# Cross-attention and routed FFN on one core: where twelve output-projection pieces, four residual adds and one key product stand in the steps of a batch

## The chip, the cores and the metric

One Trainium2 chip, one of its cores. The metric is the device time of the kernel in microseconds (us). The engines are TensorE (PE in the rows; PEld is its weight load), VectorE (DVE), ScalarE (ACT), GpSimd (POOL) and SyncE (SP), which here only issues transfers.

## The reference

```python
# B=8 batches of S=512 tokens, H=512, 16 heads of 32, context width 128
x = x + xattn(layernorm(x), ctx)          # causal attention, keys and values from ctx
x = x + ffn(layernorm(x))                 # router of 8 experts, top 2 by output column

def xattn(q, latent):
    qp = q @ Wq.T;  k, v = split(latent @ Wkv.T)
    scores = (qh @ kh.T) / sqrt(32), masked to the causal part
    out = softmax(scores) @ vh
    return out @ Wout.T
```

Every matrix product of float32 is made of three products of a high and a low part.

## The kernel before, in words

The first third of the span is the attention, the rest the router and the experts. The change touches only the attention.

The attention runs over 8 batches. A batch is four groups `c` = 0 to 3 of four heads each (called first to fourth group here), and a group is eight steps `v` = 0 to 7 (`UNITS`). The order of work is written out by hand: each engine's `body` is one Python loop over `c` and `v`, and small tables and functions say which extra pieces stand in which step. Engines meet only through semaphores. In each step TensorE makes, in this order:

- `shifted_scores` (L705): the transposed scores of one block of keys for two heads, into the one pair of banks `e_ps`. It waits until ScalarE has taken the exponential (L1095) of the step before. In step 0 it also waits for `rows_in`: two rows of row maxima that SyncE has copied into the stacked operands (L380).
- The score product of the second head for the group ahead (L672), whose row maxima VectorE takes (L1390; L1384 where the mask is added on TensorE by L678). TensorE may write a score bank again when `negmax` has counted the maxima that read it.
- Extra pieces: a quarter of a query product in steps 0, 2, 3 and 4; in step 1 the rest of the previous group's values and sums (L721, L741); in step 7 the first two blocks of values (L721, L733); a key product (`keys`) in step `key_step(c)`.
- The output projection of the **previous** batch (`project_out`, three matmuls at L261 to L263 with the operands `wo_h`, `wo_l`, `oT_h`, `oT_l`). A batch has 4 row blocks `i` of 4 pieces. All four pieces of a block add up in the one bank `j_ps[0]`. The first piece of the next block waits (`take(0, ...)`, `freed`) for `x1_ok`, which counts VectorE's `residual` (L1426): the add of the old `x` that empties this bank.
- The score product of the first head (or the masked pair), and in step 5 `turn_maxima` (L687), which transposes the maxima of the next group.

After L687 ScalarE and VectorE split the transposed maxima (L1020, `lo_shift` at L1399, which stands behind the maxima of step 5), SyncE copies the two rows (L380), and step 0 of the next group may begin.

Which piece stands where: `OUT_FIRST` gives the first of four steps in a row for each block. `summed_block` gives the step of the residual, one after the block's last piece; VectorE makes it ahead of the maxima of that step. The key product of the fourth group stands in step 5 and its low part (`lo_of`, L1372) in step 6 (`key_rest`), ahead of the maxima. Keys of the first and fourth group use `j_ps[0]` too, the same bank as the output projection. The first batch has no projection, and the last batch has tables of its own (`OUT_FIRST_LAST`), which the change leaves alone, so six of the eight batches have the four blocks of the table `OUT_FIRST`.

Of the kernel before, what the change touches and what calls it, by code (L numbers as in the profile page):

```python
# [34 lines left out]
UNITS = QB * 2  # L35
# [10 lines left out]
def build(nc, x, ctxT, wqT, wkvT, woT, routerT, router_b, expertT, expert_b, out):  # L46
    ctx = ExitStack()
    with ctx:
# [170 lines left out]
        def some(value):  # L219

            return not isinstance(value, int) or value > 0
# [43 lines left out]
        def target(c, v):  # L265

            k = v + LEAD
            return 1 + k // UNITS, k % UNITS

        def masked(c, v):  # L270

            return v in (3, 4) or c == 0 and v > 4

        def block_of(v):

            return QB - 1 - v // 2
# [18 lines left out]
        def key_bank(c):  # L295

            return 1 if c in (1, 2) else 0

        def key_step(c):

            return 6 if c in (1, 2) else 5

        OUT_FIRST = ((1, 0), (1, 6), (2, 3), (3, 0))
        OUT_FIRST_LAST = ((1, 0), (1, 4), (2, 0), (2, 4))

        def key_rest(c):

            return {0: (0, 5), 1: (1, 7), 2: (2, 7), 3: (3, 6)}[c]

        FIX_EXPERT = 1  # L310
        EXPERT_FIXES = 2 * NE
# [6 lines left out]

        def out_block(c, v, last):

            for i, (c0, v0) in enumerate(OUT_FIRST_LAST if last else OUT_FIRST):
                chunk = (c - c0) * UNITS + v - v0
                if 0 <= chunk < KC:
                    return i, chunk
            return None

        def summed_block(c, v, last):

            step = c * UNITS + v - (0 if last else 1)
            at = out_block(step // UNITS, step % UNITS, last)  # L330
            return at[0] if at and at[1] == KC - 1 else None


# [275 lines left out]
        def _(pe):  # L609
# [197 lines left out]
            def body(b, first, more, further):  # L807
# [7 lines left out]
                for c in range(KC):  # L815
# [3 lines left out]
                    def project(v):  # L819
                        i, chunk = out_block(c, v, last)  # L820
                        if chunk == 0:
                            take(0, "WO", (b - 1) * QB + i)
                        project_out(b - 1, i, chunk, 0)
# [5 lines left out]
                    for v in range(UNITS):  # L829
# [19 lines left out]
                        if v == key_step(c) and ahead:  # L849
                            take(key_bank(c), "K", n + AHEAD)  # L850
                            keys((c + AHEAD) % KC, b if c == 0 else b + 1, key_bank(c))
# [127 lines left out]
        def _(act):  # L979
# [101 lines left out]
            def body(b, first, more, further):  # L1081
                last = not more
                for c in range(KC):
                    n = b * KC + c
                    ahead = more or c == 0
                    for v in range(UNITS):
# [22 lines left out]
                        if v == key_step(c) and ahead:  # L1109
                            hi_of(n + AHEAD, KH, "k", key_bank(c))  # L1110
# [212 lines left out]
        def _(dve):  # L1323
# [23 lines left out]
            def block_statistics(b, i):  # L1347
                if i == 0:
                    dve.wait_ge(s["x_in"], (b + 1) * 16)
                statistics(b * QB + i, i, xt[:, i, :], "ln")  # L1350
                mean_variance(b * QB + i, i, "ln")
# [5 lines left out]
            def turned_tokens(g, i, bank):  # L1357
                dve.wait_ge(s["xT_hi"], g + 1)
                cols = slice(i * P, (i + 1) * P)
                dve.tensor_tensor(xnT_l[:, :, cols], j_ps[bank][:].rearrange("p (k q) -> p k q", k=KC),  # L1360
                                  f32(xnT_h[:, :, cols]), ALU.subtract).then_inc(s["xT_lo"], 1)

            def lo_of(n, part, name, bank):

                dve.wait_ge(s[name + "_hi"], n + 1)
                full, hi = j_ps[bank], f32(qk[:, part - 1])
                if name == "q":

                    dve.scalar_tensor_tensor(qk[:, part], full[:], SCALE, hi, ALU.mult, ALU.subtract)\
                        .then_inc(s["q_lo"], 1)  # L1370
                else:
                    dve.tensor_tensor(qk[:, part], full[:], hi, ALU.subtract).then_inc(s["k_lo"], 1)  # L1372

            def maxima(n, c, v, mask=False):

                u = n * UNITS + v
                i, pair = block_of(v), v % 2
                if v == 0 and some(n - 1):

                    dve.wait_ge(s["turned"], n - 1)  # L1380
                if mask:
                    at = 2 * pair * QB + i
                    dve.wait_ge(s["scores"], 2 * u + 2)
                    dve.tensor_reduce(nmax[:, c % 2, at:at + QB + 1:QB], s_ps[:, :, 0:(i + 1) * P], AX_X, ALU.max,  # L1384
                                      negate=True).then_inc(s["negmax"], 2)
                for j in range(0 if mask else 2):
                    at = (2 * pair + j) * QB + i
                    dve.wait_ge(s["scores"], 2 * u + 1 + j)
                    row = s_ps[:, j, 0:(i + 1) * P]
                    dve.tensor_tensor_reduce(row, row, future[:, S - (i + 1) * P:S], -1.0, -MASKED, ALU.add, ALU.min,  # L1390
                                             accum_out=nmax[:, c % 2, at:at + 1]).then_inc(s["negmax"], 1)

            def lo_shift(n):

                dve.wait_ge(s["nm_hi"], n + 1)
                if some(n * (16 * SHIFT_ROWS)):
                    dve.wait_ge(s["rows_in"], n * (16 * SHIFT_ROWS))
                rows = slice(0, HC * QB)
                dve.tensor_tensor(nm_l[rows, :], r_ps, f32(nm_h[rows, :]), ALU.subtract).then_inc(s["nm_lo"], 1)  # L1399

            def refined(n, c):

                dve.wait_ge(s["recips"], n + 1)
                o = o_sb[OUT_BUF[c]]
                dve.scalar_tensor_tensor(d_ps[:], d_ps[:], -1.0, o[:], ALU.mult, ALU.mult).then_inc(s["refined"], 1)
                dve.wait_ge(s["refined"], 2 * n + 1)
                dve.scalar_tensor_tensor(o[:], d_ps[:], 2.0, o[:], ALU.add, ALU.mult).then_inc(s["refined"], 1)

            def scaled(n, c, totals=o_ps):

                dve.wait_ge(s["refined"], (n + 1) * 2)
                o = o_sb[OUT_BUF[c]]
                dve.tensor_tensor(o[:], totals[:], o[:], ALU.mult).then_inc(s["o_ok"], 1)
# [9 lines left out]
            def residual(b, i, bank):  # L1423
                dve.wait_ge(s[f"xr_in{i % 2}"], (b * (QB // 2) + i // 2 + 1) * 16)
                dve.wait_ge(s["wo_mm"], b * QB + i + 1)
                dve.tensor_tensor(xr[:, i % 2, :], j_ps[bank][:], xr[:, i % 2, :], ALU.add).then_inc(s["x1_ok"], 1)  # L1426
# [32 lines left out]
            def body(b, first, more, further):  # L1459
                last = not more  # L1460
                for c in range(KC):
                    n = b * KC + c
                    ahead = more or c == 0
                    for v in range(UNITS):
                        if v == TURN + 1 and (more or c < KC - 1):
                            lo_shift(n + 1)
                        if not (first and c == 0):
                            if v == REFINED:
                                refined(n - 1, (c - 1) % KC)
                            if v == SCALED:  # L1470
                                scaled(n - 1, (c - 1) % KC)
                        i = None if first else summed_block(c, v, last)
                        if i is not None:
                            residual(b - 1, i, 0)
                        if (c, v) == key_rest(c) and ahead:
                            lo_of(n + AHEAD, KL, "k", key_bank(c))
                        if c == 0 and more:
                            for i in TURNED.get(v, ()):
                                turned_tokens((b + 1) * QB + i, i, 1 - i % 2)
                        if (c, v) in STATISTICS and further:  # L1480

                            block_statistics(b + 2, STATISTICS.index((c, v)))
                        g, vv = target(c, v)
                        if more or c + g < KC:
                            maxima(n + g, (c + g) % KC, vv, masked(c, v))
                        if QUERY.get(v) == KC - 1 and ahead:
                            lo_of(n + AHEAD, QL, "q", 1)
                        if last:
                            for k, q in FIX_EARLY.get((c, v), ()):
                                fix_router(k, q)  # L1490
                        if last and (c, v) in LO_EARLY:
                            lo_router(LO_EARLY.index((c, v)))
# [71 lines left out]
            def lo_router(e):  # L1564
                dve.wait_ge(s["fw_hi"], e + 1)
                dve.tensor_tensor(w_l[:, e], w_raw[:, e], f32(w_h[:, e]), ALU.subtract).then_inc(s["fw_lo"], 1)
# [392 lines left out]
```

## Time and profile before

| | |
|---|---|
| time, median of 3 runs | 1985.36 us (1985.3 to 1987.68) |
| the profiled execution, its own time | 1986.06 us |
| its span | 1984.3 us |
| TensorE busy | 1910.6 us, 96% |
| VectorE busy | 1432.1 us, 72% |
| ScalarE busy | 1039.0 us, 52% |
| GpSimd busy | 850.5 us, 43% |
| TensorE weight load busy | 1514.7 us, 76% |

The span runs from the first to the last instruction of one profiled execution, and its own time is that of the same execution. Busy shares are means over stages with different limits; the last product of scores and values in the attention starts at 614.8 us. A batch in its middle repeats itself within some hundredths of a microsecond, so that one batch can be read for all. The rows below are of the batch from 266.90 to 339.60 us and, where a step without a projection piece is wanted, of the first batch.

### The profile page before, as it was taken

The page shows a single profiled execution, that of the slowest core. Times are in us where ns is not written, and L with a number is a line of the kernel's source. Part 1 is how long each engine was busy: PE and PEld are TensorE (multiplying, and loading weights), DVE is VectorE, ACT ScalarE, POOL GpSimd, SP SyncE. Part 2 cuts the span into 40 slices and gives each one's busy share as a digit, 9 for nine tenths or more (in the row PEclk, how much of TensorE's full clock was granted, in tenths as well). Part 3 has the DMA queues.
Part 4 walks back from the last instruction along what each step waited for, and adds up shares of the span by engine and source line. Part 5 has one row for each costly group of instructions (what it writes and reads, how often), then busy time and mean ns, then how long its engine had stood idle before and what let it go on. Part 6 is the DMA issues. An engine that isn't in the chain of part 4 may idle for free.

```text
span 1984.3 us, 30426 instructions
## 1 busy us (share of the span) xinstructions
PE 1910.6 (96%) x9772; PEld 1514.7 (76%) x9772; DVE 1432.1 (72%) x2840; ACT 1039.0 (52%) x2062; POOL 850.5 (43%) x1016
## 2 busy tenths in 40 slices
PE   4899999999998999999999999999999999999999
PEld 3666766777765788888888888778888888888887
DVE  5667667767668658787888888477777777777732
ACT  2566566566554347877777787533443333344400
POOL 5577777777674135456445435102321111232100
PEclk8999999999999999999999999999999999999999
DMA  5454555455466468787856555822232222223111
GB/s 166 121 125 130 137 144 128 124 149 134 108 166 229 159 229 274 231 271 221 254 203 217 190 186 196 313 85 79 94 118 85 80 95 85 80 86 124 49 42 33
DMA packets 103693, 294.54 MB, mean 148 GB/s; under 512 B 13777, under 2 KB 14801, under 8 KB 98482
## 3 DMA queue, kind: packets, MB, share of 16 engines
q1 hardware_dynamic: 91394, 209.44, 33.1%
q10 hardware_dynamic: 8880, 67.37, 10.5%
q0 software_dynamic: 3328, 16.78, 3.7%
q8 instruction: 25, 0.41, 0.1%
q14 instruction: 66, 0.54, 0.1%
HBM read 150.31 MB, written 109.16 MB: 131 GB/s over the span
## 4 chain that ended last, share of the span: by engine, by line
PE 83%; DVE 7%; DMA 3%; issue 2%; POOL 2%; ACT 2%; ACTq 0%; SPq 0%; DVEq 0%; POOLq 0%
PE pair L261 20%; PE pair L263 20%; PE pair L262 20%; PE pair L672 3%; PE ps L721 3%; PE ps L261 3%; PE pair L705 3%; PE ps L262 3%; PE ps L263 3%; DMA w_raw<-w_fix 1%; DVE pair L1390 1%; PE ps L741 1%; DVE w_raw L1525 1%; POOL pT L1836 1%; PE ps L902 1%
## 5 line engine op out<-in xcount | busy, mean ns | idle before, releaser
L261 PE MATMUL pair<-w_h,hT 128*128 128x512 f32 x1920 | 751.7, 392 | 6.4 <-ACT w_h L1201 3.6
L263 PE MATMUL pair<-w_h,hT 128*128 128x512 f32 x1920 | 748.5, 390 | 0.0
L262 PE MATMUL pair<-w_l,hT 128*128 128x512 f32 x1920 | 748.3, 390 | 0.0
L1908 POOL TENSOR_TENSOR logits<-logits,second 128x512 f32<-128x512 f32 x224 | 298.6, 1370 | 590.9 <-DVE second L1605 590.6
L261 PEld LDWEIGHTS pair<-w_h,hT 128*128 128x128 f32 x1920 | 361.4, 188 | 81.9 <-issue 5.8
L263 PEld LDWEIGHTS pair<-w_h,hT 128*128 128x128 f32 x1920 | 361.1, 188 | 75.8
L262 PEld LDWEIGHTS pair<-w_l,hT 128*128 128x128 f32 x1920 | 361.3, 188 | 74.1
L1708 DVE SCALAR_TENSOR_TENSOR xb<-pair,c_all,xb 128x512 f32<-128x512 f32 x256 | 191.7, 749 | 195.6 <-PE pair L263 189.5
L1095 ACT ACTIVATE pT<-pair,zero 128x1024 f32<-128x1024 f32 (+3 forms) x256 | 202.6, 792 | 192.0 <-PE pair L705 183.6
L1390 DVE CUSTOM_DVE_ANT_0 pair<-pair,future 128x256 f32<-128x256 f32 (+3 forms) x340 | 184.1, 554 | 124.3 <-PE pair L672 115.9
L1191 ACT ACTIVATE w<-tree 128x512 f32<-128x512 f32 x32 | 20.3, 635 | 388.6 <-DVE tree L1607 388.6
L672 PE MATMUL pair<-qk_st 96*128 96x256 f32 (+3 forms) x512 | 159.3, 341 | 21.7 <-DVE nmax L1390 7.8
L1836 POOL TENSOR_SCALAR_AFFINE_SELECT pT<-pT 128x256 f32<-128x256 f32 x248 | 105.6, 426 | 137.1 <-ACT pT L1095 136.8
L1659 DVE SCALAR_TENSOR_TENSOR scrap<-ps,w 128x512 bf16<-128x512 f32 x224 | 152.9, 683 | 0.8 <-ACT w L1194 0.8
L1170 ACT ACTIVATE over<-over 128x512 f32<-128x512 f32 x224 | 141.7, 633 | 7.0
L1167 ACT ACTIVATE junk<-over 128x512 bf16<-128x512 f32 x224 | 141.5, 632 | 7.1
L1653 DVE SCALAR_TENSOR_TENSOR ps<-logits,ps 128x512 f32<-128x512 f32 x192 | 133.2, 694 | 16.3
L672 PEld LDWEIGHTS pair<-qk_st 96*128 96x128 f32 x512 | 96.8, 192 | 62.9 <-issue 23.9
L705 PE MATMUL pair<-qk_st 98*128 98x256 f32 (+3 forms) x512 | 133.2, 341 | 8.3 <-ACT pT L1095 6.3
L1162 ACT ACTIVATE over<-logits 128x512 f32<-128x512 f32 x224 | 130.2, 624 | 8.6 <-POOL logits L1908 7.6
L1828 POOL TENSOR_TENSOR acc<-acc,pT 128x512 f32<-128x512 f32 (+1 forms) x124 | 125.2, 1010 | 10.3
L1823 POOL TENSOR_TENSOR acc<-pT,pT 128x768 f32<-128x768 f32 x62 | 114.4, 1846 | 5.2
(166 smaller groups left out, 2609.7 us busy)
## 6 DMA issues: line engine op xcount, KB each, us to landing
logits<-lg_all ACTq DMA_DIRECT2D x32, 1792.0 KB, 8.9
qk_st<-qk SPq DMA_DIRECT2D x372, 128.0 KB, 2.4
lg_all<-ev_a SPq DMA_DIRECT2D x31, 768.0 KB, 8.5
lg_all<-ev_b SPq DMA_DIRECT2D x31, 768.0 KB, 3.8
xb<-x SPq DMA_DIRECT2D x64, 256.0 KB, 2.9
hT_all<-hT SPq DMA_DIRECT2D x32, 512.0 KB, 4.3
hT<-hT_all SPq DMA_DIRECT2D x32, 512.0 KB, 4.0
xt<-in_x SPq DMA_DIRECT2D x8, 1024.0 KB, 5.4
```

The lines of the kernel that those rows point to most:

```text
L261: pe.matmul(dst, lh, rh, start=start, stop=False)
L262: pe.matmul(dst, lh, rl, start=False, stop=False)
L263: return pe.matmul(dst, ll, rh, start=False, stop=stop)
L672: mm = pe.matmul(s_ps[:, j, 0:w], qk_st[c][0:STACK, 0, hh, i * P:w], qk_st[c][0:STACK, 1, hh, 0:w], start=True, stop=not mask)
L705: mm = pe.matmul(dst[:, j, 0:w], qk_st[c][0:STACK + SHIFT_ROWS, 1, hh, kb * P:(kb + 1) * P], qk_st[c][0:STACK + SHIFT_ROWS, 0, hh, kb * P: ...
L1095: act.activation(pT[kb][:, pair:pair + 2, :], src[:, :, 0:S - kb * P], ACT.Exp, bias=zero[:])\
L1167: act.activation(junk[:], over[j][:], ACT.Sign, accum_out=sign_sum[:, i, e:e + 1])\
L1170: act.activation(over[j][:], over[j][:], ACT.Tanh, scale=0.5, accum_out=tanh_sum[:, i, e:e + 1]).then_inc(s["first_step"], 1)
L1390: dve.tensor_tensor_reduce(row, row, future[:, S - (i + 1) * P:S], -1.0, -MASKED, ALU.add, ALU.min, accum_out=nmax[:, c % 2, at:at + 1]).t ...
L1659: dve.scalar_tensor_tensor(scrap[:, e % 2, :], taken_ps[e % 2], 1.0, w2[:], ALU.min, ALU.mult, accum_out=c_taken[:, i, e - 1:e]).then_inc( ...
L1708: dve.scalar_tensor_tensor(xb[i][:], l_ps[e % 4], c_all[:, t, e:e + 1], xb[i][:], ALU.mult, ALU.add).then_inc(s["acc"], 1)
L1908: pool.tensor_tensor(logits[t % 2][:, e - 1, :], logits[t % 2][:, e - 1, :], second[:], ALU.subtract)\
```

## The change

Blocks 0 to 3 are the row blocks of the output projection. `(c, v)` is group index and step.

| | before | after |
|---|---|---|
| block 0, pieces | (1,0) (1,1) (1,2) (1,3) | the same |
| block 0, residual | (1,4), ahead of the maxima | (1,4), behind the maxima |
| block 1, pieces | (1,6) (1,7) (2,0) (2,1) | (1,6) (1,7) (2,0) (2,2) |
| block 1, residual | (2,2), ahead | (2,3), behind |
| block 2, pieces | (2,3) (2,4) (2,5) (2,6) | (2,4) (2,5) (2,6) (2,7) |
| block 2, residual | (2,7), ahead | (3,0), behind |
| block 3, pieces | (3,0) (3,1) (3,2) (3,3) | (3,1) (3,2) (3,3) (3,4) |
| block 3, residual | (3,4), ahead | (3,5), ahead |
| keys of the fourth group | (3,5), low part (3,6) | (3,6), low part (3,7) |

Counted by step, (2,1), (2,3) and (3,0) lose a piece and (2,2), (2,7) and (3,4) get one. Nothing is added or left out.

```diff
         def key_step(c):
 
-            return 6 if c in (1, 2) else 5
-
-        OUT_FIRST = ((1, 0), (1, 6), (2, 3), (3, 0))
+            return 6 if c else 5
+
+        OUT_AT = (((1, 0), (1, 1), (1, 2), (1, 3)), ((1, 6), (1, 7), (2, 0), (2, 2)),
+                  ((2, 4), (2, 5), (2, 6), (2, 7)), ((3, 1), (3, 2), (3, 3), (3, 4)))
+        SUMMED_AT = ((1, 4), (2, 3), (3, 0), (3, 5))
...
-            return {0: (0, 5), 1: (1, 7), 2: (2, 7), 3: (3, 6)}[c]
+            return {0: (0, 5), 1: (1, 7), 2: (2, 7), 3: (3, 7)}[c]
...
-            for i, (c0, v0) in enumerate(OUT_FIRST_LAST if last else OUT_FIRST):
+            if not last:
+                for i, steps in enumerate(OUT_AT):
+                    if (c, v) in steps:
+                        return i, steps.index((c, v))
+                return None
+            for i, (c0, v0) in enumerate(OUT_FIRST_LAST):
...
-            step = c * UNITS + v - (0 if last else 1)
-            at = out_block(step // UNITS, step % UNITS, last)
+            if not last:
+                return SUMMED_AT.index((c, v)) if (c, v) in SUMMED_AT else None
+            at = out_block(c, v, last)
...
-                        i = None if first else summed_block(c, v, last)
-                        if i is not None:
-                            residual(b - 1, i, 0)
+                        summed_i = None if first else summed_block(c, v, last)
+                        sooner = last or (c, v) == (3, 5)
+                        if summed_i is not None and sooner:
+                            residual(b - 1, summed_i, 0)
...
                             maxima(n + g, (c + g) % KC, vv, masked(c, v))
+                        if summed_i is not None and not sooner:
+                            residual(b - 1, summed_i, 0)
```

In the rows below, line numbers of the changed kernel are 8 higher than those of before (L1434 is the residual L1426, L713 is L705 and so on).

VectorE, third group, from step 2 to step 4, before: the residual of block 1 stands ahead of the second pair of maxima.

```order
L1426 TENSOR_TENSOR xr<-ps,xr 128x512
L1390 ISA pair,nmax<-pair,future 128x256
L1390 ISA nmax 128x1
L1390 ISA pair,nmax<-pair,future 128x256
L1390 ISA nmax 128x1
L1405 SCALAR_TENSOR_TENSOR ps<-ps,o_sb_90 128x512
L1407 SCALAR_TENSOR_TENSOR o_sb_90<-ps,o_sb_90 128x512
L1384 TENSOR_REDUCE nmax<-pair 128x2
L1413 TENSOR_TENSOR o_sb_90<-ps,o_sb_90 128x512
L1384 TENSOR_REDUCE nmax<-pair 128x2
```

The same place in the changed kernel:

```order
L1398 ISA pair,nmax<-pair,future 128x256
L1398 ISA nmax 128x1
L1398 ISA pair,nmax<-pair,future 128x256
L1398 ISA nmax 128x1
L1413 SCALAR_TENSOR_TENSOR ps<-ps,o_sb_90 128x512
L1415 SCALAR_TENSOR_TENSOR o_sb_90<-ps,o_sb_90 128x512
L1392 TENSOR_REDUCE nmax<-pair 128x2
L1434 TENSOR_TENSOR xr<-ps,xr 128x512
L1421 TENSOR_TENSOR o_sb_90<-ps,o_sb_90 128x512
L1392 TENSOR_REDUCE nmax<-pair 128x2
```

The residual now stands behind the two operations that refine the reciprocals (L1413, L1415 there) and behind the masked maxima of step 3 (L1392).

TensorE, third group, from `shifted_scores` of step 7 to that of the fourth group's step 0, before:

```order
L705 MATMUL pair<-qk_st_75 128x128 x2
L672 MATMUL pair<-qk_st_73 128x512
L721 MATMUL ps<-pT_77,v_sb 32x512 x4
L733 MATMUL ps<-pT_77,ones 32x128 x4
L721 MATMUL ps<-pT_78,v_sb 32x384 x4
L671 ISA
L672 MATMUL pair<-qk_st_73 128x384
L696 REGISTER_ALU
L705 MATMUL pair<-qk_st_76 128x512 x2
```

And in the changed kernel:

```order
L713 MATMUL pair<-qk_st_75 128x128 x2
L680 MATMUL pair<-qk_st_73 128x512
L729 MATMUL ps<-pT_77,v_sb 32x512 x4
L741 MATMUL ps<-pT_77,ones 32x128 x4
L729 MATMUL ps<-pT_78,v_sb 32x384 x4
L261 MATMUL ps<-wo_h,oT_h 128x512
L262 MATMUL ps<-wo_l,oT_h 128x512
L263 MATMUL ps<-wo_h,oT_l 128x512
L679 ISA
L680 MATMUL pair<-qk_st_73 128x384
L704 REGISTER_ALU
L713 MATMUL pair<-qk_st_76 128x512 x2
```

The last piece of block 2 has come in between the values of step 7 (L729) and the score product.

VectorE, fourth group, from the masked maxima of step 3 to the split of the turned maxima (`nm_l`), before:

```order
L1384 TENSOR_REDUCE nmax<-pair 128x2
L1413 TENSOR_TENSOR o_sb_91<-ps,o_sb_91 128x512
L1426 TENSOR_TENSOR xr<-ps,xr 128x512
L1384 TENSOR_REDUCE nmax<-pair 128x2
L1369 SCALAR_TENSOR_TENSOR qk<-ps,qk 128x512
L1390 ISA pair,nmax<-pair,future 128x512
L1390 ISA nmax 128x1
L1390 ISA pair,nmax<-pair,future 128x512
L1390 ISA nmax 128x1
L1399 TENSOR_TENSOR nm_l<-ps,nm_h 16x128
```

And in the changed kernel:

```order
L1392 TENSOR_REDUCE nmax<-pair 128x2
L1421 TENSOR_TENSOR o_sb_91<-ps,o_sb_91 128x512
L1392 TENSOR_REDUCE nmax<-pair 128x2
L1377 SCALAR_TENSOR_TENSOR qk<-ps,qk 128x512
L1434 TENSOR_TENSOR xr<-ps,xr 128x512
L1398 ISA pair,nmax<-pair,future 128x512
L1398 ISA nmax 128x1
L1398 ISA pair,nmax<-pair,future 128x512
L1398 ISA nmax 128x1
L1407 TENSOR_TENSOR nm_l<-ps,nm_h 16x128
```

The residual of block 3 has moved from ahead of the masked maxima of step 4 to ahead of the maxima of step 5, right behind the low part of the queries (L1377).

## Rows read from the trace of the kernel before

**Rows 1.** Third group: length; busy PE, PEld, DVE, ACT, POOL (instructions); clock, DMA share, GB/s.

```profile
305.04:322.59 17.55, 17.34 (x119) 12.64 (x119) 13.72 (x40) 9.71 (x14) 12.98 (x22) 1.00 0.49 121
```

**Rows 2.** Timeline of PE, second group's step 7, third group: start us, us, engine, line.

```profile
301.65 0.34 PE L705 MATMUL pair<-qk_st 98*128 98x128 f32 x2
...
305.04 0.63 PE L705 MATMUL pair<-qk_st 98*128 98x512 f32 x2
...
307.24 0.63 PE L705 MATMUL pair<-qk_st 98*128 98x512 f32 x2
...
310.33 0.52 PE L705 MATMUL pair<-qk_st 98*128 98x384 f32 x2
...
314.34 0.45 PE L705 MATMUL pair<-qk_st 98*128 98x256 f32 x2
...
315.33 0.39 PE L261 MATMUL ps<-wo_h,oT_h 128*128 128x512 f32 x1
...
316.41 0.45 PE L705 MATMUL pair<-qk_st 98*128 98x256 f32 x2
...
319.91 0.34 PE L705 MATMUL pair<-qk_st 98*128 98x128 f32 x2
...
322.59 0.63 PE L705 MATMUL pair<-qk_st 98*128 98x512 f32 x2
```

**Rows 3.** Timeline of PE, fourth group of the same batch.

```profile
324.80 0.63 PE L705 MATMUL pair<-qk_st 98*128 98x512 f32 x2
...
326.97 0.50 PE L261 MATMUL ps<-wo_h,oT_h 128*128 128x512 f32 x1
...
327.89 0.52 PE L705 MATMUL pair<-qk_st 98*128 98x384 f32 x2
...
332.12 0.45 PE L705 MATMUL pair<-qk_st 98*128 98x256 f32 x2
...
333.50 0.51 PE L705 MATMUL pair<-qk_st 98*128 98x256 f32 x2
334.06 0.50 PE L261 MATMUL ps<-ctx_h,wkv_h 128*128 128x512 f32 x1
...
339.60 0.72 PE L705 MATMUL pair<-qk_st 98*128 98x512 f32 x2
```

**Rows 4.** Timeline of PE, first batch (no projection), fourth group, steps 0 to 2.

```profile
106.12 0.72 PE L705 MATMUL pair<-qk_st 98*128 98x512 f32 x2
...
108.05 0.72 PE L705 MATMUL pair<-qk_st 98*128 98x512 f32 x2 [0.16 <-ACT pT L1095]
...
110.53 0.52 PE L705 MATMUL pair<-qk_st 98*128 98x384 f32 x2
```

**Rows 5.** Timeline of DVE, third and fourth group, same batch as rows 2 and 3.

```profile
316.68 0.42 DVE L1384 TENSOR_REDUCE nmax<-pair 128x2 f32<-128x256 f32 x1 [1.03 <-PE pair L678]
317.02 0.68 DVE L1369 SCALAR_TENSOR_TENSOR qk<-ps,qk 128x512 fp32r<-128x512 f32 x1
...
325.65 0.57 DVE L1390 CUSTOM_DVE_ANT_0 pair<-pair,future 128x384 f32<-128x384 f32 x1
...
332.73 0.68 DVE L1413 TENSOR_TENSOR o_sb<-ps,o_sb 128x512 f32<-128x512 f32 x1
333.32 0.68 DVE L1426 TENSOR_TENSOR xr<-ps,xr 128x512 f32<-128x512 f32 x1
...
335.41 0.70 DVE L1390 CUSTOM_DVE_ANT_0 pair<-pair,future 128x512 f32<-128x512 f32 x1 [0.48 <-PE ps L687]
...
336.67 0.27 DVE L1399 TENSOR_TENSOR nm_l<-ps,nm_h 16x128 fp32r<-16x128 f32 x1
```

**Rows 6.** Transfers of the shift rows, fourth group: the issue, and issue to landing.

```profile
337.63 0.59 SPq L380 DMA_DIRECT2D qk_st<-nm_l  x1
...
DMA to landing us min/median/max: 1.8/1.8/1.8
```

## The prediction

> **What bounds the kernel now.** I read the page first: TensorE is busy nearly all the time, so the question is what a step of the attention waits for. Busy time by stretch says less than it seems: in the third group of a batch TensorE shows 17.34 of 17.55 us busy, VectorE 13.72, at a granted clock of 1.00 [rows 1]. So I took the timeline of TensorE and read the start of every L705, which opens a step. The difference of two neighbours is what a step costs, waits included, and the same step with and without a projection piece gives the price of a piece there. Then I read VectorE's timeline beside it, since TensorE stops where `negmax` or `x1_ok` is late, and SyncE's issues, since a group cannot begin before its two shift rows have landed.
>
> What the reader is to see. Step 1 lasts 3.09 us with a piece (307.24 to 310.33) [rows 2] and 2.48 without (108.05 to 110.53) [rows 4]. Step 0 lasts 2.21 us with a piece (322.59 to 324.80) [rows 2, 3] and 1.93 without (106.12 to 108.05), and there the next step waits for ScalarE's exponential [rows 4], so part of the piece is covered. Step 4 lasts 2.07 us with a piece (314.34 to 316.41) [rows 2] and 1.38 without (332.12 to 333.50) [rows 3]. Step 7 lasts 3.39 us with a piece (301.65 to 305.04) and 2.68 without (319.91 to 322.59) [rows 2]. The price of a piece is thus 0.28 us in step 0, 0.61 in step 1, 0.69 in step 4 and 0.71 in step 7. The change moves pieces out of the cheap places and into the dear ones.
>
> The fourth group ends on something else. VectorE's split of the maxima ends at 336.94 (336.67 and 0.27) [rows 5], the second shift row is issued at 337.63 and lands 1.8 later, at 339.43 [rows 6], and the next group's step 0 starts at 339.60 [rows 3]. So there the end of the group follows L1399 at 2.66 us, whatever TensorE does meanwhile. From step 5 to the end that group takes 6.10 us (333.50 to 339.60) [rows 3] with one key product in it, the third group 6.18 (316.41 to 322.59) [rows 2] with three extra pieces: TensorE has room there.
>
> **The change part by part, for one batch.** No instruction and no transfer is added or removed, so every term is a place.
>
> *Block 0, second group.* Its residual goes behind the maxima of step 4. The next steps there are held by the exponentials and the low part of the queries, and VectorE does the same sum of work before the maxima of step 5. I take 0.
>
> *Third group, step 1* loses its piece: 3.09 to 2.48, a gain of 0.61.
>
> *Third group, steps 2 to 4* last 6.08 us together now (310.33 to 316.41) [rows 2], with pieces in steps 3 and 4. After the change the pieces are in steps 2 and 4, which would be no longer. But the piece of step 4 is the first of block 2 and must wait for the residual of block 1, and this now stands behind the refined reciprocals and the masked maxima. I time this chain on the fourth group, whose step 2 has a piece already: step 2 starts at 327.89 [rows 3], and what stands behind the masked maxima of step 3 (there L1413) starts at 332.73 [rows 5], 4.84 later. In its place comes the residual, 0.68 long, and TensorE goes on 0.06 after a residual: L1426 ends at 334.00 [rows 5] and the product that waited for it starts at 334.06 [rows 3]. So the piece starts 4.84 + 0.68 + 0.06 = 5.58 after step 2's start. From that piece to the next step is 1.08 (315.33 to 316.41) [rows 2]. The stretch becomes 6.66, a loss of 0.58. It eats what step 1 gave. Bounds: without a wait 6.08 or a little less (0), and 0.7 more if VectorE is late there by one operation.
>
> *Third group, steps 5 to 7.* Steps 5 and 6 keep their pieces. Step 7 gets one behind the values: 2.68 to 3.39, a loss of 0.71. The rows of the third group have landed long before. Bounds: 0 if something covers it, 0.71 as read in the second group. I take 0.71, since that step is the same but for the group. The residual that stood in this step is gone from it, but nobody waited there for it.
>
> Third group together: -0.61 + 0.58 + 0.71 = +0.68 us.
>
> *Fourth group, step 0* loses its piece: 2.21 to 1.93, a gain of 0.28. *Step 1* keeps one, now the first of block 3, which waits for the residual of block 2 behind the maxima of step 0. The second of these maxima starts 0.85 after step 1's start (325.65 against 324.80), VectorE's operations of that kind follow at 0.6 or less, and the residual with its 0.68 ends some 2.1 to 2.2 after it; the piece stands at 2.17 (326.97) [rows 3, 5]. It just fits, and I take 0.
>
> *Fourth group, step 4* gets a piece: 1.38 to 2.07, a loss of 0.69. Step 5 then starts 0.41 later than now.
>
> *Fourth group, steps 5 to 7.* The end is that of L1399, so I follow VectorE from the start of step 5. Now the maxima of step 5 start 1.91 after it (335.41 against 333.50) [rows 3, 5]. Then: the masked maxima of step 4 start 0.27 after it (316.68 against 316.41, a step 4 with a piece), the low part of the queries 0.34 later (317.02) [rows 2, 5], and two operations, this one and the residual, at the distance of 0.59 that L1413 and L1426 show (332.73 to 333.32) [rows 5]: 0.27 + 0.34 + 2 x 0.59 = 1.79. That is 0.12 sooner. Before, TensorE's key product had itself waited for the residual (until 334.06) [rows 3] and held up the score; that goes away. Maxima, L1399, rows and landing follow as before. The key product now lies in step 6 beside this leg; TensorE's room there covers it, and if it did not it would cost the 0.69 of a product of three matmuls.
>
> Fourth group together: -0.28 + 0.69 - 0.12 = +0.29 us.
>
> *SyncE and the key operands.* The residuals of blocks 1 and 3 end later, and their stores stand ahead of the shift rows in SyncE's queue. Block 3's ends 1.88 after step 5's start and L1399 some 1.4 later, so the store of one issue is out before. The key's low part comes two maxima later, about 1.26 us (335.41 to 336.67) [rows 5]. Behind it are twelve copies of heads, at 0.59 an issue and 1.8 to land [rows 6] 8.9 us, read first after step 5 of the next group, which starts over 11 us into a group (305.04 to 316.41) [rows 2]. Both cost 0.
>
> **Sum.** 0.68 + 0.29 = 0.97 us a batch, and six batches have these tables: +5.8 us. The first batch only gets the moved keys, in the same cover, and the last nothing. The profiled execution took 1986.06 us around its span of 1984.3; with 5.8 it would be 1991.9. The median of the runs is 0.7 lower, 1985.36, and gives 1991.2 us.
>
> **The rivals.** What tells a measurement of this kernel from no change is 0.2%, 4.0 us or 0.66 us a batch.
>
> *A. TensorE does not wait at the third group's step 4.* If VectorE gets the residual of block 1 done in time, the 0.58 goes: 0.39 a batch, +2.3, 1987.7 us, no change that can be told. It decides from a wait shorter by 0.31. Against it stands the order of the rows: two refinements and the masked maxima are ahead of it, and they are timed. Chance 0.10.
>
> *B. The piece in step 7 is covered.* TensorE's weight loads fill only 12.64 of 17.55 us in the third group, against 17.34 of its matmuls [rows 1]. If the engine has that room, the piece of step 7 costs nothing: 0.26 a batch, +1.6, 1987.0 us. Against it, a piece in this very step of the second group costs 0.71 [rows 2]. Chance 0.13. The Trainium skill, Perfetto Trace Analysis, section Identifying the Most-Contended Engine, speaks for this rival: it calls matmul busy time a poor measure because matmuls are pipelined, and wants the busy share of the weight loads instead. By that rule the engine has headroom in which moved work should vanish; by the steps with and without a piece it has not, in steps 1, 4 and 7, and I go by those.
>
> *C. More waits.* At the fourth group's step 1 the margin is nil. If the residual of block 2 slips behind one more operation of some 0.5 us, each batch loses that too: +8.8, 1994.2 us. Chance 0.12.
>
> *D. Faster.* It would need A and B at once and more: together they give 0.97 - 0.58 - 0.71 = -0.32 a batch, -1.9 us, still within 0.2%. Only if the fourth group's piece in step 4 were covered too (-0.69) would it be -6.1, 1979.3. Chance 0.06. That the new order does not take effect is excluded by the order of instructions, but its effect may be lost in what I do not see: 0.03.
>
> My forecast has 0.56. The range goes from 1986.8, which takes in A and B, to 1994.6, which takes in C. Slower has my forecast and C, 0.68; the same A, B and the rest, 0.26; faster 0.06.
>
> **What the profile of the changed kernel would show.** L705 starts of the batch: the third group about 18.2 us long (17.55 now), the fourth about 17.3 (17.01). Step 1 of the third group 2.5 us, its step 7 3.4. In its step 4 TensorE idle some 0.6 to 0.7 us before the L261 with `wo_h`, released by the residual. In the fourth group step 0 near 1.9, step 4 near 2.1, the maxima of step 5 right behind the residual, and the second shift row landing just before the next step 0. The first and second group unchanged. I am wrong if the wait is absent, or if step 7 stays at 2.7.

## The result, and the profile after

The changed kernel takes 1994.58 us, median of 6 runs (1993.91 to 1997.54), against 1985.73 us for the kernel before (6 runs). The ratio is 1.0043, 95% interval 1.0033 to 1.0053: slower, by 8.5 us by the ratio and 8.85 us between the medians. I had said 1991.2 us, in a range from 1986.8 to 1994.6.

The page of the changed kernel, its head and first part: span, then busy time, share of the span and instructions of each engine.

```profile
span 1992.4 us, 30426 instructions
## 1 busy us (share of the span) xinstructions
PE 1917.2 (96%) x9772; PEld 1513.1 (76%) x9772; DVE 1431.7 (72%) x2840; ACT 1039.6 (52%) x2062; POOL 847.6 (43%) x1016
```

The same instructions, and a span 8.1 us longer than 1984.3. To see where, I read one batch in its middle, the same batch as in the rows of before. Busy time by stretch: length, busy PE, PEld, DVE, ACT, POOL, then clock, DMA share and GB/s. First the second group before, then the second, third and fourth group of the changed kernel.

```profile
286.28:305.04 18.76, 17.55 (x120) 12.58 (x119) 12.53 (x32) 9.34 (x14) 13.04 (x16) 1.00 0.56 152
```

```profile
289.11:308.23 19.12, 17.96 (x120) 12.57 (x119) 12.53 (x32) 9.33 (x14) 13.01 (x16) 1.00 0.52 149
308.23:326.35 18.12, 17.63 (x119) 12.64 (x119) 13.20 (x39) 9.71 (x14) 12.98 (x22) 1.00 0.45 117
326.35:343.83 17.48, 16.86 (x113) 11.47 (x113) 13.59 (x40) 11.93 (x18) 13.24 (x22) 1.00 0.48 122
```

The third group was 17.55 us [rows 1] and is 18.12, the fourth was 17.01 and is 17.48. The second, whose pieces did not move at all, was 18.76 and is 19.12. That is 0.57 + 0.47 + 0.36 = 1.40 us in this batch, and six times that would be 8.4 us. The clock is 1.00 in all three.

The six batches together, before and changed:

```profile
121.40:557.08 435.68, 421.14 (x2894) 306.55 (x2893) 307.40 (x822) 265.97 (x404) 325.18 (x454) 1.00 0.52 133
```

```profile
121.49:565.34 443.85, 426.99 (x2892) 305.92 (x2892) 306.62 (x822) 266.23 (x404) 325.41 (x456) 1.00 0.51 130
```

They are 8.17 us longer, against 8.1 us between the spans: that is the whole loss. The batch read is near the mean of the six (1.36), but they repeat less exactly than I had said ahead of the prediction: before, the second group takes 18.76 to 18.87 us in the first five of the six and 18.45 in the last, and in the changed kernel 19.09 to 19.25 and 18.69.

Timeline of TensorE of the changed kernel, steps 5 to 7 of the second group and then the third group. L713 opens a step (it was L705).

```profile
300.98 0.50 PE L713 MATMUL pair<-qk_st 98*128 98x256 f32 x2
...
302.34 0.44 PE L713 MATMUL pair<-qk_st 98*128 98x128 f32 x2
...
303.12 0.49 PE L261 MATMUL ps<-ctx_h,wkv_h 128*128 128x512 f32 x1
...
304.84 0.34 PE L713 MATMUL pair<-qk_st 98*128 98x128 f32 x2
...
310.42 0.63 PE L713 MATMUL pair<-qk_st 98*128 98x512 f32 x2
...
312.82 0.52 PE L713 MATMUL pair<-qk_st 98*128 98x384 f32 x2
...
316.58 0.51 PE L713 MATMUL pair<-qk_st 98*128 98x256 f32 x2
...
318.25 0.50 PE L261 MATMUL ps<-wo_h,oT_h 128*128 128x512 f32 x1 [0.47 <-DVE xr L1434]
...
319.45 0.45 PE L713 MATMUL pair<-qk_st 98*128 98x256 f32 x2
...
322.96 0.34 PE L713 MATMUL pair<-qk_st 98*128 98x128 f32 x2
...
326.35 0.63 PE L713 MATMUL pair<-qk_st 98*128 98x512 f32 x2
```

Step 1 of the third group takes 2.40 us (310.42 to 312.82). The stretch from step 2 to step 5 takes 6.63 (312.82 to 319.45), with the wait for the residual in it, which the trace names at 318.25. Step 7 takes 3.39 (322.96 to 326.35). What I had not foreseen is step 6 of the second group: 2.50 us (302.34 to 304.84) where it was 2.18 (299.47 to 301.65 [rows 2]). TensorE and VectorE of the kernel before there:

```profile
299.47 0.44 PE L705 MATMUL pair<-qk_st 98*128 98x128 f32 x2
...
300.03 0.40 PE L261 MATMUL ps<-ctx_h,wkv_h 128*128 128x512 f32 x1
```

```profile
297.93 0.68 DVE L1426 TENSOR_TENSOR xr<-ps,xr 128x512 f32<-128x512 f32 x1
...
298.86 0.68 DVE L1369 SCALAR_TENSOR_TENSOR qk<-ps,qk 128x512 fp32r<-128x512 f32 x1
```

There the low part of the queries (L1369) ended 0.07 us after step 6 had begun (299.54), and the key product started 0.56 after it. VectorE's timeline shows what is late now. Changed kernel, steps 5 and 6 of the second group:

```profile
301.25 0.43 DVE L1392 TENSOR_REDUCE nmax<-pair 128x2 f32<-128x256 f32 x1 [0.36 <-PE pair L686]
301.59 0.68 DVE L1434 TENSOR_TENSOR xr<-ps,xr 128x512 f32<-128x512 f32 x1
302.19 0.68 DVE L1377 SCALAR_TENSOR_TENSOR qk<-ps,qk 128x512 fp32r<-128x512 f32 x1
302.79 0.69 DVE L1398 CUSTOM_DVE_ANT_0 pair<-pair,future 128x512 f32<-128x512 f32 x1
```

The residual (L1434) has gone behind the maxima (L1392), as the change says, and so ahead of the low part of the queries (L1377). That ends at 302.87, 0.53 us after step 6 has begun. The key product of step 6 (L261 with `ctx_h`) uses bank 1, which the queries must have left: it starts at 303.12, 0.78 after step 6 has begun. How the 0.25 us between 302.87 and 303.12 come about stays open: a product that waited for a residual started 0.06 after it [rows 3, 5], and the trace names no releaser here.

The fourth group, TensorE and then VectorE of the changed kernel:

```profile
328.34 0.73 PE L713 MATMUL pair<-qk_st 98*128 98x512 f32 x2 [0.32 <-ACT pT L1103]
...
331.54 0.51 PE L713 MATMUL pair<-qk_st 98*128 98x384 f32 x2
...
335.77 0.45 PE L713 MATMUL pair<-qk_st 98*128 98x256 f32 x2
...
337.83 0.45 PE L713 MATMUL pair<-qk_st 98*128 98x256 f32 x2
```

```profile
338.44 0.68 DVE L1377 SCALAR_TENSOR_TENSOR qk<-ps,qk 128x512 fp32r<-128x512 f32 x1
339.04 0.68 DVE L1434 TENSOR_TENSOR xr<-ps,xr 128x512 f32<-128x512 f32 x1
339.64 0.69 DVE L1398 CUSTOM_DVE_ANT_0 pair<-pair,future 128x512 f32<-128x512 f32 x1
...
340.89 0.27 DVE L1407 TENSOR_TENSOR nm_l<-ps,nm_h 16x128 fp32r<-16x128 f32 x1
```

Step 0 takes 1.99 (326.35 to 328.34) and waits for ScalarE, step 1 takes 3.20, step 4 takes 2.06. The maxima of step 5 (L1398) start 1.81 after that step (339.64 against 337.83), right behind the residual. The split of the turned maxima ends at 341.16, and the next group starts 2.67 later, at 343.83: this group ends with its shift rows as before [rows 3, 6].

### The profile page after: what moved, and what is told of

Same layout as the page of the kernel before. It is cut to its first block, busy times and chain, and to the rows that moved or that the text cites. A ratio compares the mean times of both kernels' runs of the same rounds, so it can differ in the third digit from the quotient of the medians.

```text
span 1992.4 us, 30426 instructions
## 1 busy us (share of the span) xinstructions
PE 1917.2 (96%) x9772; PEld 1513.1 (76%) x9772; DVE 1431.7 (72%) x2840; ACT 1039.6 (52%) x2062; POOL 847.6 (43%) x1016
## 4 chain that ended last, share of the span: by engine, by line
PE 86%; DVE 6%; DMA 3%; ACT 2%; issue 2%; POOL 1%; ACTq 0%; SPq 0%; DVEq 0%; POOLq 0%
PE pair L261 20%; PE pair L263 20%; PE pair L262 20%; PE pair L680 4%; PE ps L261 4%; PE pair L713 4%; PE ps L729 4%; PE ps L262 3%; PE ps L263 3%; DMA w_raw<-w_fix 1%; DVE nmax L1392 1%; PE ps L749 1%; ACT pT L1103 1%; DVE w_raw L1536 1%; PE ps L910 1%
## 5 line engine op out<-in xcount | busy, mean ns | idle before, releaser
L261 PE MATMUL pair<-w_h,hT 128*128 128x512 f32 x1920 | 751.5, 391 | 6.4 <-ACT w_h L1209 2.8
L261 PEld LDWEIGHTS pair<-w_h,hT 128*128 128x128 f32 x1920 | 360.9, 188 | 82.2 <-issue 6.2
L1398 DVE CUSTOM_DVE_ANT_0 pair<-pair,future 128x256 f32<-128x256 f32 (+3 forms) x340 | 184.0, 554 | 124.2 <-PE pair L680 120.4
L713 PE MATMUL pair<-qk_st 98*128 98x256 f32 (+3 forms) x512 | 132.2, 339 | 8.1 <-ACT pT L1103 6.4
```

Source lines behind the costliest of these rows:

```text
L261: pe.matmul(dst, lh, rh, start=start, stop=False)
L713: mm = pe.matmul(dst[:, j, 0:w], qk_st[c][0:STACK + SHIFT_ROWS, 1, hh, kb * P:(kb + 1) * P], qk_st[c][0:STACK + SHIFT_ROWS, 0, hh, kb * P: ...
```

## The experiments

There were eight runs. Each ran beside the kernel before on its chip, whose median was 1986.87 us beside the runs with block 0's residual ahead, with block 1's ahead, with the keys alone and with the pieces in the cheap steps, and 1986.08 us beside the other four. The ratios are to these. Since the times of a kernel spread over several us, I read the group lengths of one batch in the middle first and the time second. An edit is against the changed kernel unless it says otherwise.

**Block 0's residual ahead again** (the changed kernel with one edit)

```diff
-                        sooner = last or (c, v) == (3, 5)
+                        sooner = last or (c, v) in ((1, 4), (3, 5))
```

> The changed kernel with one edit: block 0's residual stands ahead of the maxima of step 4 again; all else stays moved. Theory Q (queue on VectorE): the second group's step 6 grew by 0.31 to 0.39 us because the low part of the queries now stands behind the residual, and the key product of step 6 waits for it. Then step 6 falls from 2.50 back to 2.2 us, the second group from 19.12 to 18.8, and the time is 2.0 us under the changed kernel, about 1992.5 (ratio to before 1.0034). Rival P (the second group is longer for another reason, as a phase between GpSimd and TensorE that the other moves set up): step 6 stays at 2.5 and the time at 1994.6.

The second group, by stretch:

```profile
292.51:311.31 18.80, 17.59 (x119) 12.58 (x119) 12.53 (x32) 9.34 (x14) 13.03 (x16) 1.00 0.56 152
```

It is 18.80, and the third and fourth group stay at 18.11 and 17.48. Step 6 is back at 2.19. Putting the residual behind the maxima cost the second group all it lost. The timed runs cannot tell: 1994.45 us, ratio 1.0037 (1.0024 to 1.0050), where the changed kernel has 1.0043 and 1.0034 was expected.

**The low part of the queries ahead of the residual**, which stays behind the maxima

```diff
-                        if summed_i is not None and not sooner:
-                            residual(b - 1, summed_i, 0)
                         if QUERY.get(v) == KC - 1 and ahead:
                             lo_of(n + AHEAD, QL, "q", 1)
+                        if summed_i is not None and not sooner:
+                            residual(b - 1, summed_i, 0)
```

> The changed kernel with one edit: in the second group's step 4 the low part of the queries comes before block 0's residual, which stays behind the maxima. The maxima of step 5 start no sooner than in the changed kernel. Theory Q (it is the low part of the queries that the key product of step 6 waits for): step 6 falls from 2.50 to about 2.2 us and the second group from 19.12 to 18.8, though the maxima stay late. Rival X (it is the maxima of step 5, pushed back by the residual, that hold up step 6): step 6 stays at 2.5 us. In time: 1992.5 against 1994.6.

VectorE in steps 5 and 6 of the second group, and the group by stretch:

```profile
302.36 0.68 DVE L1377 SCALAR_TENSOR_TENSOR qk<-ps,qk 128x512 fp32r<-128x512 f32 x1
302.96 0.68 DVE L1434 TENSOR_TENSOR xr<-ps,xr 128x512 f32<-128x512 f32 x1
303.56 0.69 DVE L1398 CUSTOM_DVE_ANT_0 pair<-pair,future 128x512 f32<-128x512 f32 x1
```

```profile
289.87:308.69 18.82, 17.72 (x120) 12.44 (x119) 12.52 (x32) 9.32 (x14) 13.05 (x16) 1.00 0.54 152
```

The maxima are as late as in the changed kernel, 1.81 us after step 5 begins, and the group is back at 18.82. Step 6 is back at 2.19. So it is the place of the low part of the queries that counts; the key product is what the kernel makes wait for it. Rival X falls. Time 1993.95 us, ratio 1.0044 (1.0028 to 1.0061), where about 1992.5 us was expected.

This order has a price of its own. The third group is 18.20 here, 0.08 longer than in the changed kernel, and SyncE's issues in the second group show why:

```profile
303.67 0.35 SPq L422 DMA_DIRECT2D x<-xr  x1
305.68 0.33 SPq L418 DMA_DIRECT2D xr<-in_x  x1
306.11 0.57 SPq L388 DMA_DIRECT2D qk_st<-nm_h  x1
306.72 0.59 SPq L388 DMA_DIRECT2D qk_st<-nm_l  x1
```

The residual ends at 303.64, its store (L422) is issued behind it, the load into the same buffer (L418) waits for that store, and the shift rows stand behind both in SyncE's queue. The second row lands 1.9 us after its issue, at 308.6, and the third group starts at 308.69. In the changed kernel it was issued at 305.36 and landed 0.9 us before the group's start. In the fifth of the six batches of this run the second group takes 19.12 us; there the trace names the second shift row as what the next step waited for.

**Block 1's residual ahead of the masked maxima**

```diff
-                        sooner = last or (c, v) == (3, 5)
+                        sooner = last or (c, v) in ((2, 3), (3, 5))
```

> The changed kernel with one edit: block 1's residual at the third group's step 3 stands ahead of the masked maxima, not behind them. Theory W (the piece at step 4 waits for exactly this residual): it starts 0.34 us sooner, step 4 falls from 2.87 to about 2.5 us, the third group from 18.12 to about 17.8, the time by 2.0 us to about 1992.6. Rival M (then the masked maxima are late instead and TensorE waits for their counter before the score of step 4): the third group stays within 0.1 of 18.12 and the time at 1994.6.

The third group:

```profile
307.59:325.36 17.77, 17.61 (x120) 12.65 (x120) 13.20 (x39) 9.71 (x14) 12.93 (x22) 1.00 0.47 119
```

Step 4 fell from 2.87 to 2.54, the group to 17.77: theory W, as expected. The time is 1990.77 us, ratio 1.0022 (1.0012 to 1.0032), against 1.0043; about 1992.6 us was expected.

**Both residuals ahead**

```diff
-                        sooner = last or (c, v) == (3, 5)
+                        sooner = last or c in (1, 2) or (c, v) == (3, 5)
```

> The changed kernel with the residuals of blocks 0 and 1 both ahead of the maxima (the other two as in the changed kernel). If the two waits are independent, both repairs add: second group 18.8, third 17.78, fourth 17.47, 73.4 us a batch against 72.72 before and 74.11 changed, time about 1990.2 (ratio to before 1.0021); what is left over before is the price of the moved places alone. If one wait hides the other, the sum is less: 73.7 or more a batch.

```profile
287.64:306.47 18.83, 17.59 (x120) 12.59 (x119) 12.53 (x32) 9.33 (x14) 13.02 (x16) 1.00 0.54 151
306.47:324.23 17.76, 17.60 (x120) 12.65 (x119) 13.20 (x39) 9.71 (x14) 12.92 (x22) 1.00 0.47 120
```

The fourth group stays at 17.48. The two repairs add: 73.47 us for this batch, first group included, against 74.10 changed and 72.70 before. The time is 1990.77 us, ratio 1.0025 (1.0014 to 1.0036), no lower than with block 1's residual ahead alone; the timed runs do not resolve the second repair. Just under half of the loss (0.63 of 1.40 us a batch) is where two residuals stand in VectorE's queue; the rest is the places of the pieces, net of what the keys gain (below).

**A piece left out.** The kernel before without one piece of the second group's step 7; that quarter of block 1's sum is missing from the output.

```diff
-                        if out and not (c == 1 and v == 0):
+                        if out and not (c == 1 and v == 0) and (last or (c, v) != (1, 7)):
                             project(v)
```

> The kernel before without the projection piece of the second group's step 7 in batches 1 to 6 (three matmuls a batch, the second quarter of block 1's sum: left out of the computation). My price: step 7 falls from 3.39 to 2.7 us, the second group from 18.77 to about 18.06, the time by 4.2 us to about 1981.5 (ratio 0.9979). Rival B of the prediction (pieces in step 7 lie in TensorE's own room): less than 0.2 us a group, the time within 1 us of before.

```profile
286.86:304.93 18.07, 16.86 (x116) 12.01 (x116) 12.53 (x32) 9.33 (x14) 12.78 (x16) 1.00 0.56 158
```

The group is 18.07, and its step 7 is 2.68 us where it was 3.39. A piece in step 7 costs its full 0.7 us. 1982.64 us, ratio 0.9986 (0.9976 to 0.9996); 4.2 us had been expected and 3.4 were measured, by the medians, against the kernel before beside it. Rival B of the prediction falls, as the third group's own step 7 says too (3.39 where it was 2.68), and with it the reading that I had made of the Trainium skill, Perfetto Trace Analysis, section Identifying the Most-Contended Engine: a weight load that is busy 12.64 of 17.55 us in the third group [rows 1] did not mean that TensorE had room in its step 7. The page judges headroom by that share and by the FLOPs against the peak; I had taken the first alone.

**The fourth group's part alone**

```diff
-        OUT_AT = (((1, 0), (1, 1), (1, 2), (1, 3)), ((1, 6), (1, 7), (2, 0), (2, 2)),
-                  ((2, 4), (2, 5), (2, 6), (2, 7)), ((3, 1), (3, 2), (3, 3), (3, 4)))
-        SUMMED_AT = ((1, 4), (2, 3), (3, 0), (3, 5))
+        OUT_AT = (((1, 0), (1, 1), (1, 2), (1, 3)), ((1, 6), (1, 7), (2, 0), (2, 1)),
+                  ((2, 3), (2, 4), (2, 5), (2, 6)), ((3, 1), (3, 2), (3, 3), (3, 4)))
+        SUMMED_AT = ((1, 4), (2, 2), (2, 7), (3, 5))
...
-                        sooner = last or (c, v) == (3, 5)
+                        sooner = True
```

> The fourth group's part of the change alone: block 3's pieces in steps 1 to 4, its residual in step 5 ahead of the maxima, keys one step on; blocks 0 to 2 and their residuals as before. If the fourth group's loss is its own: 17.47 us as in the changed kernel, other groups as before (18.77, 17.55), time +2.8 us, 1988.5 (ratio 1.0014), and against the run with the keys alone (16.63) the piece brought into step 4 then costs 0.8 us net. If instead it comes from block 2's residual standing behind the maxima of step 0: 17.35 or less.

```profile
325.88:343.38 17.50, 16.87 (x114) 11.48 (x113) 13.05 (x40) 11.92 (x18) 13.22 (x22) 1.00 0.48 122
```

The fourth group is 17.50, the second 18.76 and the third 17.54. Its loss is its own, and block 2's residual behind the maxima of step 0 has no part in it. 1988.76 us, ratio 1.0017 (1.0007 to 1.0027).

**The keys alone one step on** (the kernel before)

```diff
-            return 6 if c in (1, 2) else 5
+            return 6 if c else 5
...
-            return {0: (0, 5), 1: (1, 7), 2: (2, 7), 3: (3, 6)}[c]
+            return {0: (0, 5), 1: (1, 7), 2: (2, 7), 3: (3, 7)}[c]
```

> The kernel before with the fourth group's keys alone moved one step on (product to step 6, low part to step 7); pieces and residuals stay where they were. Theory L (the fourth group ends with the landing of the shift rows, and the key product that waits for the residual in step 5 holds up the score whose maxima stand ahead of the split): the maxima of step 5 start about 0.4 us sooner, the fourth group falls from 17.01 to about 16.65, in six batches 2.1 us, 1983.6 (ratio 0.9990). Rival N (the product costs its 0.7 us in step 6, where it now stands on TensorE's own path, as keys in step 6 do in the other groups): the fourth group stays at 17.0 or grows, 1985.7 or more.

```profile
322.22:338.85 16.63, 16.24 (x114) 11.49 (x113) 13.23 (x40) 11.92 (x18) 12.34 (x20) 1.00 0.50 128
```

16.63 against 17.01: this part of the change is a gain of 0.38 us a batch. The maxima of step 5 start 1.53 us after the step in this trace, where it was 1.91, the split ends at 336.18, and the next group starts 2.67 after it (338.85). The product in step 6 lies in the time that the shift rows take anyway; theory L holds. Set against it, the run before this one shows what block 3 alone costs, with its piece out of step 0 and into step 4 and its residual in step 5: 0.87 net (17.50 - 16.63). In time, 1985.07 us, ratio 0.9992 (0.9983 to 1.0000), which alone would settle nothing.

**Pieces in the cheap steps**, with the keys one step on

```diff
-        OUT_AT = (((1, 0), (1, 1), (1, 2), (1, 3)), ((1, 6), (1, 7), (2, 0), (2, 2)),
-                  ((2, 4), (2, 5), (2, 6), (2, 7)), ((3, 1), (3, 2), (3, 3), (3, 4)))
-        SUMMED_AT = ((1, 4), (2, 3), (3, 0), (3, 5))
+        OUT_AT = (((1, 0), (1, 1), (1, 2), (1, 3)), ((1, 5), (1, 6), (1, 7), (2, 0)),
+                  ((2, 2), (2, 3), (2, 4), (2, 5)), ((3, 0), (3, 1), (3, 2), (3, 3)))
+        SUMMED_AT = ((1, 4), (2, 1), (2, 6), (3, 4))
...
-                        sooner = last or (c, v) == (3, 5)
+                        sooner = True
```

> The kernel's pieces at other steps again, by the prices read: block 0 in the second group's steps 0 to 3, block 1 in its steps 5, 6, 7 and the third group's step 0, block 2 in steps 2 to 5, block 3 in the fourth group's steps 0 to 3; residuals ahead of the maxima in the second group's step 4, the third group's steps 1 and 6, the fourth group's step 4; keys one step on as in the changed kernel. Against before, the third group loses its pieces in steps 1 (0.61) and 6 (0.70) and gets one in step 2 (0.32), the second group gets one in step 5 (some 0.25). Theory L and the prices: third group about 16.8 us (then it ends with its shift rows), second about 19.0, fourth about 16.65; 0.9 us a batch less than before, 1980.3 (ratio 0.997). Rival (the new residuals hold up maxima or the shift rows of the third group, and the piece in step 5 costs its full 0.7): 1984 to 1986.

```profile
283.73:302.75 19.02, 18.14 (x122) 13.13 (x122) 12.53 (x32) 9.32 (x14) 13.07 (x16) 1.00 0.52 150
302.75:319.28 16.53, 16.53 (x117) 12.05 (x116) 13.60 (x40) 9.61 (x14) 12.58 (x22) 1.00 0.52 128
319.28:336.02 16.74, 16.36 (x113) 11.59 (x113) 13.19 (x39) 11.93 (x18) 12.69 (x21) 1.00 0.50 127
```

19.02, 16.53 and 16.74, where 19.0, 16.8 and 16.65 were expected: the third group gained 0.27 more than I had priced. The batch is 71.70 us, 1.00 less than before. 1979.92 us, ratio 0.9965 (0.9952 to 0.9977): this version beats both kernels. The same sixteen pieces stand in it, but five of them in steps 1, 4, 6 and 7, where before has seven and the changed kernel eight, and the third group now ends with its shift rows too (the second is issued at 317.39 and lands 1.8 later, and the next group starts at 319.28).

**The six batches in every trace.** This is one execution of each kernel; the last column compares medians of the timed runs with the kernel before beside them.

| | six batches, us | against before | in time |
|---|---|---|---|
| before | 435.68 | | |
| changed | 443.85 | +8.17 | +8.85 |
| block 0's residual ahead | 441.95 | +6.27 | +7.58 |
| low part of the queries ahead | 443.02 | +7.34 | +7.87 |
| block 1's residual ahead | 441.68 | +6.00 | +3.90 |
| both residuals ahead | 439.94 | +4.26 | +4.69 |
| fourth group alone | 438.42 | +2.74 | +2.68 |
| keys alone | 433.87 | -1.81 | -1.80 |
| a piece left out | 431.93 | -3.75 | -3.44 |
| pieces in the cheap steps | 429.76 | -5.92 | -6.95 |

Each run stands where six times its batch read puts it, within about half a microsecond. The timed runs differ from this by up to 2.1 us.

## Why the prediction was right, and where its sum was off

The direction and most of the mechanism held: pieces went out of cheap steps into dear ones, and one of them met a wait that had not been there. That the time lies in the range is luck: 1994.58 is 0.02 us below the upper end, which was set for rival C, and rival C did not come. The sum of 0.97 us a batch was too small; it is 1.40 in the batch read. Term by term:

*Third group, step 1:* -0.61 said, -0.69 measured (2.40 against 3.09).

*Third group, steps 2 to 4:* +0.58 said, +0.55 measured (6.63 against 6.08). The piece started 5.43 us after step 2, not 5.58, and the next step 1.20 after it, not 1.08; the product that waited shows 0.50 us in its row, where the same one showed 0.39 before [rows 2]. TensorE's row shows 0.47 us idle ahead of it, not 0.6 to 0.7. The run with this residual ahead shows that it is this wait: the piece starts 0.33 sooner. Rival A falls.

*Third group, step 7:* +0.71 said, +0.71 measured, and the run without a piece confirms the price. Rival B falls.

*Fourth group:* +0.29 said, +0.47 measured. Step 4 (+0.68) and the way to the split (3.06 us after step 5 instead of 3.17, so -0.11 against my -0.12) are as said. Off are step 0, -0.22 instead of -0.28, since the exponential ends it at 1.99 and not at 1.93, and step 1, +0.11 where I had 0. I had feared a wait for the residual of block 2 there (rival C). The trace does name this residual as the releaser of the piece's weight load:

```profile
330.61 0.19 PEld L261 LDWEIGHTS ps<-wo_h,oT_h 128*128 128x128 f32 x1 [0.62 <-DVE xr L1434]
```

But with the fourth group's part alone this residual is done long before, and the weight load stands at the same 2.27 us after step 1's start and the step takes the same 3.20. So it was not this wait. What both runs show is that `shifted_scores` of step 1 had waited for the exponential and took 0.73 us where it took 0.63 [rows 3]; that this is the 0.11 is argued, not shown.

*Second group:* 0 said, +0.36 measured. **This is the step that failed**: "VectorE does the same sum of work before the maxima of step 5. I take 0." The sum of work is the same, but not its order. The first half of that sentence even names the low part of the queries among what holds the next steps, but the residual went ahead of this low part, and I asked only who waits for the maxima. The key product of step 6 waits for the low part, through the bank that it shares with the queries: the step takes 2.50 us where it took 2.18. Two runs, one with the residual ahead and one with the low part ahead, both take the group back to 18.8. My forecast that the second group would be unchanged is wrong by this.

*SyncE:* 0 said, and in the changed kernel the terms above leave nothing for it. But I looked at the residuals of blocks 1 and 3 only; the run with the low part of the queries ahead shows that block 0's, one operation later still, pushes the shift rows to the end of the second group.

*The rest:* between the two profiled executions the first batch differs by -0.7 us and the last by +1.0. What stands ahead of the first and behind the last, by +0.8 and -1.2, nearly evens that out.

Of the 8.17 us of the six batches the sum had 5.8. Most of what was missing is the second group, 2.0 us over the six.

## What to carry to other kernels

An instruction that is put behind another on an engine's queue is put ahead of a third; when you cost such a move, list everything between the old place and the new one and ask of each who waits for it, also through a shared bank, and what the moved instruction's own transfers stand ahead of.

In a schedule written out by hand, the price of a piece is not its own duration but the difference of the same step with it and without it. Here it was 0.7 us in steps that TensorE fills itself, and 0.2 to 0.3 in steps that end with a wait, and a table of these prices led to a version 0.35% faster than before.

Where groups repeat, compare the lengths of groups in one trace; effects of 0.3 us a group were plain there, which the timed runs did not resolve. Read all the repeats before you multiply one: in the changed kernel the second group differed by up to 0.16 us between five of the six batches, and by more in the last.

## What the runs showed of the hardware

The first and the last batch of the attention are not as steady as the six between them. From its first step to the start of the second batch, the first batch took between 66.35 us (changed kernel) and 70.19 (block 0's residual ahead). In the latter the granted clock was down in the first stretches (0.68 from 54 to 70 us, where the changed kernel shows 0.86 from 55 to 70). Busy time by stretch, with block 0's residual ahead:

```profile
54.00:70.00 16.00, 14.98 (x55) 12.17 (x55) 6.48 (x24) 7.63 (x11) 6.17 (x8) 0.68 0.48 116
```

In the changed kernel's last batch, TensorE was busy 1.28 of 3 us around step 6 of its first group, and then the granted clock was 0.57:

```profile
578.00:581.00 3.00, 1.28 (x10) 1.06 (x8) 2.01 (x3) 1.52 (x4) 2.83 (x5) 1.00 0.32 55
581.00:584.00 3.00, 3.00 (x25) 1.34 (x27) 1.23 (x1) 0.47 (x1) 2.48 (x4) 0.57 1.01 353
```

With block 1's residual ahead, whose last batch has the same order of work, the same place kept the clock:

```profile
576.00:579.00 3.00, 1.29 (x10) 1.07 (x8) 2.01 (x3) 1.52 (x4) 2.83 (x5) 1.00 0.36 61
579.00:583.00 4.00, 3.03 (x33) 1.59 (x31) 2.09 (x2) 0.48 (x1) 2.49 (x4) 1.00 0.97 335
```

So did the kernel before: 0.99 us busy of 2.70, then 1.00. Step 7 took 4.50 us in the changed kernel and 3.53 in the kernel before, so the same gap went with about 1 us in one execution and with nothing in another. Why the clock fell in one and not in the other stays open, and so does whether it is the execution or the kernel, since there is one trace of each. The tables of these two batches are not part of the change, apart from the first batch's keys.
